# Low parts of experts 5 to 7 moved behind the attention loop, its tail reordered, and one-pass count products

## The chip, the core and the metric

The kernel runs on one core of a Trainium2 chip. Its engines work side by side, each through its own list of instructions in order, and wait for one another by semaphores: TensorE (PE, with its weight loads as PEld), VectorE (DVE), ScalarE (ACT), GpSimd (POOL) and SyncE (SP), which issues transfers. The metric is the time of one execution on the device, in microseconds, as the median of several runs.

## What is computed

The input is 16 images of 16 x 16 positions with 192 channels, 4096 tokens. Three blocks follow one another, each added to its input:

```python
xs = gelu(x @ W1.T + b1)                # 192 -> 48
xs = abs(ifft2(fft2(xs) * low_mask))    # low pass over the 16 x 16 positions
x = x + xs @ W2.T + b2
t = x.reshape(16, 256, 192)
n = layernorm(t)
q, k, v = n @ Wq + bq, n @ Wk + bk, n @ Wv + bv     # 12 heads of 16; one k, one v head
t = t + softmax(rope(q) . rope(k) * scale) @ v      # over the heads of one token
n = layernorm(t)
p = softmax(n @ gate_w.T)               # 8 experts
p1, p2, e1, e2 = top2(p)                # gates p1 / (p1 + p2), p2 / (p1 + p2)
t = t + sum over the two: gate * ((silu(n @ G[e]) * (n @ U[e])) @ D[e])    # 192 -> 384 -> 192
```

As there is one key and one value head and the sum runs over the key heads of the same token, attention is a product of each token with itself. Results are float32; many products are made from a high part in fp32r and a low part (the rest), so that several one-pass products stand for one float32 product.

## The kernel before

The kernel is a hand-written program: each engine's list is written out, with its waits. The tokens lie in 32 tiles of 128, four tiles to a quad, eight quads (`QUADS`, numbered 0 to 7; `last` is 7). There are three phases, each a block that all engines leave together before the next begins.

**The front phase** (`front_phase`) makes the low pass block and then attention. Its attention loop runs over the quads, n = 0 to 7, on every engine. PE projects quad n + 1 (`project`), transposes quad n + 2 (`turn`), makes the gate logits of quad n - 4 (`logits`) and transposes the normalised rows of quad n - 3 (`turn_route`). DVE makes the scores of quad n (`scores`), adds attention to the rows of quad n - 1 and takes their statistics (`residual`), and makes the weights of quad n from ACT's exponentials (`weights`: L756, L758, L761). POOL rotates the key of quad n + 1 (`rotate_key`), weighs the value of quad n (`weigh_value`, L640) and makes the deviation and shift of quad n - 1 (`deviation`, L650 to L659). ACT copies out of PSUM, exponentiates (`exponential`), normalises rows for the gate (`norm_route`, L513, four instructions a quad) and copies logits into `lg` (`copy_logits`, L495). SP stores the normalised rows and the base of the output.

Into this loop the preparation of the experts' weights is woven. For each of the 8 experts ACT makes high parts: `wa_hi` and `wb_hi` (gate and up weights, 128 x 768 each; ACT's `split`) and the first half of `wd` (down weights, 128 x 576; ACT's `split_down`). The low parts are subtractions: `wa` by POOL's `split` (L613), `wb` by DVE's `split` (L729), and the down weights by POOL's `split_down` (L619) for experts 0 to 4 and by DVE's `split_down` (L734) for 5 to 7. POOL makes the `wa` of experts 0 to 3 ahead of the loop and 4 to 7 in its steps 0 to 3, then the down parts of 0 to 3 in steps 4 to 7 and of 4 at the end. DVE makes the `wb` of expert 0 ahead of the loop and of n + 1 in step n, and the down parts at the end of step 7 and behind the last residual.

**The tail of the front phase** finishes the gate logits of quads 4 to 7. When those of quads 0 to 5 are in `lg` (`EARLY`, 24 tiles) DVE makes the early choice (`choose_experts` on these tiles): its maximum and first subtraction (L843) let ACT exponentiate (L563); probabilities, the two best experts, `both` (which of the 8 experts are chosen, 0 or 1) and the gates follow, some twenty small instructions in a chain. ACT's list orders its end of the work: normalise quad 6, copy the logits of 4, copy quad 5's transposes out of PSUM, copy the logits of 5, exponentiate for the early choice, normalise 7, and then 6 and 7 in turn.

**The routing phase** (`routing_phase`) makes the choice for the last 8 tiles, then counts with two products over `both` (L960 with a triangle of ones for the places, L961 with a square of ones for the totals), and from these the order of the tokens by expert (`idx_map`). **The experts' phase** gathers 71 tiles of 128 rows, runs them through their experts and adds the results to the output.

Of the kernel before, what the change touches and what calls it, by code (L numbers as in the profile page):

```python
# [54 lines left out]
EPS = 1e-5  # L55
WARM = 4
ROUTE_APART = (5, 7)
SCALE = HD ** -0.5
# [29 lines left out]
def program(nc, x, xT, w1, w2, lowpass, wqkv, cos, sin, gate, wgu, down, tri, ident, iotas, ytab, out):  # L88
# [4 lines left out]
    with ExitStack() as whole:  # L93
# [41 lines left out]
        with ExitStack() as middle:  # L135
            choice = [middle.enter_context(nc.sbuf_tensor(n, [P, TILES, EXPERTS], F32)) for n in ("pr", "m1", "m2", "both", "gates", "desc")]
            front_phase(nc, early, xs, shift, rstd, eye, wa_hi, wb_hi, w_lo, wd, wqa, wqb, cos_t, sin_t, gate_w, lg, choice, rows, row_tiles,
                        x, xT, w1, w2, lowpass, wgu, down, ytab, ident, wqkv, gate, rope, iotas[1], out)
            routing_phase(nc, lg, choice, tri, iotas, row_tiles, idx_map, tile_exp, switch, out, scattered)
# [19 lines left out]
def front_phase(nc, early, xs, shift, rstd, eye, wa_hi, wb_hi, w_lo, wd, wqa, wqb, cos_t, sin_t, gate_w, lg, choice, rows, row_tiles,  # L159
# [6 lines left out]
    with ExitStack() as stack:  # L166
# [62 lines left out]
        with nc.Block() as block:  # L229
# [65 lines left out]
            def _(pe):  # L295
# [123 lines left out]
                for n in range(QUADS):  # L419
# [6 lines left out]
                    if n >= LAG:  # L426
                        turn_route(n - LAG)
                for q in range(QUADS - LAG, QUADS):
                    turn_route(q)
                    logits(q - 1)  # L430
                logits(last)

            @block.scalar
            def _(act):
# [58 lines left out]
                def copy_logits(q):  # L493
                    act.wait_ge(lg_mm_done, made(q))
                    nc.scalar.activation(lg[:, bass.ts(q, QT), :],  # L495
                                         route_banks(q)[1][:, bass.ds(2 * P, QT * EXPERTS)].rearrange("p (t e) -> p t e", t=QT),
                                         ACT.Copy).then_inc(lg_done, 1)
# [42 lines left out]
                for n in range(QUADS):  # L540
# [15 lines left out]
                    for e in DOWN_AT.get(n, ()):  # L556
                        split_down(e)
                norm_route(last - 1)
                copy_logits(last - 3)
                route_out_of_psum(last - 2)  # L560
                copy_logits(last - 2)
                act.wait_ge(early_less, 1)
                nc.scalar.activation(pr[:, 0:EARLY], lg[:, 0:EARLY], ACT.Exp).then_inc(early_ex, 1)  # L563
                norm_route(last)
                route_out_of_psum(last - 1)
                copy_logits(last - 1)
                route_out_of_psum(last)
                copy_logits(last)

            @block.gpsimd  # L570
            def _(pool):
# [89 lines left out]
                for q in range(QUADS - 1):  # L661
                    in_deviation(q)
                    if 1 < q < QUADS - 2:
                        split(q - 2)
                rotate_key(0)
                in_deviation(last)
                for n in range(QUADS):
                    if n + 1 < QUADS:
                        rotate_key(n + 1)
                    if n < EXPERTS - 4:  # L670
                        split(4 + n)
                    weigh_value(n)
                    if n:
                        deviation(n - 1)
                    if n > 3:
                        split_down(n - 4)
                deviation(last)
                split_down(4)

            @block.vector  # L680
            def _(dve):
# [45 lines left out]
                def split(e):  # L727
                    dve.wait_ge(hi_done, e + 1)
                    nc.vector.tensor_tensor(wb_lo[:, e, :], wb_lo[:, e, :].bitcast(F32), wb_hi[:, e, :].bitcast(F32), ALU.subtract)  # L729

                def split_down(e):
                    dve.wait_ge(down_hi_done, e + 1)
                    low = wd[:, e, 1, :]
                    nc.vector.tensor_tensor(low, low.bitcast(F32), wd[:, e, 0, :].bitcast(F32), ALU.subtract)  # L734

# [60 lines left out]
                finish(last)  # L796
                split(0)
                for n in range(QUADS):
                    scores(n)
                    if n:  # L800
                        residual(n - 1)
                    weights(n)
                    if n + 1 < EXPERTS:
                        split(n + 1)
                    if n + 1 == QUADS:
                        split_down(5)
                residual(last)
                split_down(6)
                split_down(7)

# [63 lines left out]
def routing_phase(nc, lg, choice, tri, iotas, row_tiles, idx_map, tile_exp, switch, out, scattered):  # L874
# [3 lines left out]
    with ExitStack() as stack:  # L878
        a = Scope(nc, stack, "route")
        trit = a.sb("trit", [P, P])  # L880
        ones, zero = a.sb("ones", [P, P]), a.sb("zero", [P, C])
        io = a.sb("io", [P, P])
        first = a.sb("first", [P, E, T])
# [21 lines left out]
        diff_done, ex_done = a.sem("diff_done"), a.sem("ex_done")  # L905
        chain = a.sem("chain")
        chosen, counted, gates_done = a.sem("chosen"), a.sem("counted"), a.sem("gates_done")
# [3 lines left out]
        with nc.Block() as block:  # L911
# [20 lines left out]
            def _(act):  # L932
                act.wait_ge(diff_done, 1)
                nc.scalar.activation(pr[:, EARLY:T], lg[:, EARLY:T], ACT.Exp).then_inc(ex_done, 1)
                act.wait_ge(consts_in, 16 * len(consts))

                def token_at(i, s):
# [14 lines left out]
            def _(pe):  # L952
                pe.sem_inc(map_done, HR)
                pe.wait_ge(consts_in, 16 * len(consts))


                pe.wait_ge(chosen, 1)
                pe.wait_ge(filled, 1)
                flat = both[:].rearrange("p t e -> p (t e)")
                nc.tensor.matmul(ps_p[:, 0:T * E], trit[:], flat, start=True, stop=True)  # L960
                nc.tensor.matmul(ps_t[:, 0:T * E], ones[:], flat, start=True, stop=True).then_inc(counted, 1)  # L961

# [465 lines left out]
```

## Time and profile before

| what | us |
|---|---|
| median of 3 runs | 410.3 (410.09 to 413.22) |
| the profiled execution | 411.45 |
| its span | 409.4 |
| attention loop, first scores to last residual | 53.73 to 115.52 |
| early choice of experts | 121.87 to 130.83 |
| routing phase | from 133.1 |
| experts' phase | from 166.1 |

The profile is one execution; its times are microseconds from the start of the span. An instruction's row gives its start, its time, engine and line, the operation, what it writes and reads, with sizes (partitions x elements), how many were merged into the row, and in brackets the idle time of its engine just before and what ended it. Where an engine can't start an instruction because a port is taken, that waiting is inside the instruction's own time.

### The profile page before, as it was taken

What the parts mean: (1) busy time and instruction counts of PE and PEld (TensorE: products, weight loads), DVE (VectorE), ACT (ScalarE), POOL (GpSimd) and SP (SyncE); (2) the same over time, 40 slices, a digit from 0 to 9 for tenths busy, and PEclk for the clock granted to TensorE, in tenths of its full rate; (3) what the DMA queues carried; (4) which work ended last, traced back from release to release, by engine and by line L of the source; (5) the groups of instructions that cost most, each with busy time, mean ns of one, the idle gap of its engine ahead of it and who ended that gap; (6) DMA issues with size and microseconds to landing.
All of it is one profiled execution on the core that took longest, in us unless ns stands there. A gap on an engine that the chain in (4) does not pass through costs nothing.

```text
span 409.4 us, 8455 instructions
## 1 busy us (share of the span) xinstructions
PE 348.5 (85%) x2162; PEld 333.8 (82%) x2163; DVE 269.5 (66%) x734; ACT 220.0 (54%) x536; POOL 265.2 (65%) x273
## 2 busy tenths in 40 slices
PE   6988675997656249799999999999999999999990
PEld 5887565887656149789999999999999999999980
DVE  2477988999856799256666656665666566656650
ACT  3485655777523059145555555555555555555540
POOL 3048577868770200347878878788787888888763
PEclk9998999698555555699999999999999999999995
DMA  6999640234442400114544445444444444444432
GB/s 173 291 338 383 221 161 1 91 125 146 138 133 91 84 1 0 53 41 71 73 75 80 71 69 77 71 80 71 69 76 70 82 69 70 76 73 79 71 38 29
DMA packets 39418, 41.07 MB, mean 100 GB/s; under 512 B 13789, under 2 KB 32448, under 8 KB 39392
## 3 DMA queue, kind: packets, MB, share of 16 engines
q0 software_dynamic: 13824, 16.98, 25.5%
q1 hardware_dynamic: 25568, 23.79, 18.6%
q8 instruction: 10, 0.16, 0.2%
q14 instruction: 16, 0.13, 0.1%
HBM read 25.78 MB, written 14.98 MB: 100 GB/s over the span
## 4 chain that ended last, share of the span: by engine, by line
PE 55%; DMA 1%; issue 1%; POOLq 0%; DVE 0%; POOL 0%; ACT 0%; SPq 0%; ACTq 0%; DVEq 0%
PE moe_ps_y L1151 10%; PE moe_ps_h L1137 6%; PE moe_ps_gt L1126 3%; PE moe_ps_gt L1130 3%; PE moe_ps_gt L1127 3%; PE moe_ps_u L1126 3%; PE moe_ps_gt L1129 3%; PE moe_ps_u L1129 3%; PE moe_ps_gt L1128 3%; PE moe_ps_y L1153 3%; PE moe_ps_u L1128 3%; PE moe_ps_u L1127 3%; PE moe_ps_u L1130 3%; PE moe_ps_x L1118 2%; PE moe_ps_x L1117 2%; PE moe_ps_y L1150 2%
## 5 line engine op out<-in xcount | busy, mean ns | idle before, releaser
L1090 POOL DMA_INDIRECT out<-moe_y,idx_map x71 | 113.0, 1592 | 29.3 <-issue 19.5
L1082 POOL DMA_INDIRECT moe_xt<-rows,idx_map x71 | 69.9, 984 | 56.7 <-POOLq L911 30.5
L1234 ACT ACTIVATE moe_yy<-moe_ps_y,moe_xt 128x384 f32<-128x384 f32 x71 | 41.3, 581 | 70.7 <-PE moe_ps_y L1151 70.7
L1151 PE MATMUL moe_ps_y<-wd,moe_h_hi 128*128 x213 | 70.2, 354 | 0.6 <-DVE moe_h_lo L1297 0.6
L1305 DVE TENSOR_TENSOR moe_y<-moe_yy 128x192 f32<-128x192 f32 x71 | 25.5, 360 | 56.1 <-ACT moe_yy L1234 56.1
L1214 ACT ACTIVATE moe_x_hi<-moe_ps_x 128x256 fp32r<-128x256 f32 x71 | 27.3, 385 | 33.9 <-PE moe_ps_x L1118 33.9
L1297 DVE TENSOR_TENSOR moe_h_lo<-moe_ps_h,moe_h_hi 128x384 fp32r<-128x384 f32 x71 | 39.6, 558 | 2.7 <-ACT moe_h_hi L1226 0.5
L1151 PEld LDWEIGHTS moe_ps_y<-wd,moe_h_hi 128*128 128x128 f32 x213 | 40.2, 189 | 1.2 <-issue 1.2
L1281 DVE TENSOR_TENSOR moe_x_lo<-moe_ps_x,moe_x_hi 128x128 fp32r<-128x128 f32 x71 | 20.7, 292 | 30.9 <-ACT moe_x_hi L1214 30.9
L1291 DVE TENSOR_TENSOR moe_hid<-moe_ps_u,moe_sg 128x384 f32<-128x384 f32 x71 | 38.9, 548 | 0.0
L1153 PE MATMUL moe_ps_y<-wd,moe_h_lo 128*128 x142 | 35.5, 250 | 0.0
L1226 ACT ACTIVATE moe_h_hi<-moe_ps_h 128x384 fp32r<-128x384 f32 x71 | 34.9, 492 | 0.5 <-PE moe_ps_h L1137 0.5
L1137 PE MATMUL moe_ps_h<-eye,moe_hid 128*128 128x128 f32 x213 | 34.9, 273 | 0.0
L1220 ACT ACTIVATE moe_sg<-moe_ps_gt 128x384 f32<-128x384 f32 x71 | 34.6, 487 | 0.0
L1126 PE MATMUL moe_ps_u<-wa_hi,moe_x_hi 128*128 x71 | 29.9, 421 | 0.0
L1153 PEld LDWEIGHTS moe_ps_y<-wd,moe_h_lo 128*128 128x128 f32 x142 | 26.9, 189 | 0.0
L356 PE MATMUL front_ps_c<-wqa,front_xa 128*128 128x232 f32 x64 | 19.7, 390 | 8.3 <-ACT front_xb L476 8.3
L1137 PEld LDWEIGHTS moe_ps_h<-eye,moe_hid 128*128 128x128 f32 x213 | 25.4, 141 | 0.2
L1126 PE MATMUL moe_ps_gt<-wa_hi,moe_x_hi 128*128 x71 | 24.2, 341 | 0.7 <-DVE moe_x_hi L1284 0.7
L1130 PE MATMUL moe_ps_gt<-w_lo,moe_x_hi 128*128 x71 | 24.0, 338 | 0.0
L1129 PE MATMUL moe_ps_u<-wb_hi,moe_x_hi 128*128 x71 | 24.0, 338 | 0.0
L1128 PE MATMUL moe_ps_u<-wa_hi,moe_x_lo 128*128 x71 | 24.0, 337 | 0.0
(228 smaller groups left out, 963.1 us busy)
## 6 DMA issues: line engine op xcount, KB each, us to landing
w_lo<-in_wgu SPq DMA_DIRECT2D x8, 768.0 KB, 15.0
xs<-in_x SPq DMA_DIRECT2D x8, 388.0 KB, 8.8
rows<-front_xr SPq DMA_DIRECT2D x8, 384.0 KB, 2.7
out<-xs SPq DMA_DIRECT2D x8, 384.0 KB, 3.5
wd<-in_down SPq DMA_DIRECT2D x8, 288.0 KB, 4.5
xta<-in_xT SPq DMA_DIRECT2D x8, 256.0 KB, 5.1
moe_xt<-rows,idx_map POOLq DMA_INDIRECT x71, 2.8
out<-moe_y,idx_map POOLq DMA_INDIRECT x71, 3.6
```

The lines of the kernel that those rows point to most:

```text
L1082: nc.gpsimd.indirect_dma_start(xt[:, slot, :], None, rows.ap(), bass.IndirectOffsetOnAxis(ap=idx_map[:, j, 0:1], axis=0)).then_inc(gathere ...
L1090: nc.gpsimd.indirect_dma_start(out, bass.IndirectOffsetOnAxis(ap=idx_map[:, j, 1:2], axis=0), y[:, j % YR, :], None, compute_op=ALU.add).t ...
L1126: nc.tensor.matmul(at, x_hi[:, s, 0:P], wa_hi[:, e, w], start=True, stop=False)
L1128: nc.tensor.matmul(at, x_lo[:, s, :], wa_hi[:, e, w], start=False, stop=False)
L1129: nc.tensor.matmul(at, hb, wb_hi[:, e, w], start=False, stop=False)
L1130: nc.tensor.matmul(at, hb, w_lo[:, e, 1, w], start=False, stop=True).then_inc(done, 1)
L1137: ins = nc.tensor.transpose(ps_h[:, bass.ts(k, P)], hid[:, s, bass.ts(k, P)], eye[:])
L1151: ins = nc.tensor.matmul(both, hi, halves, start=(k == 0), stop=(k == 2))
L1153: nc.tensor.matmul(first, lo, high, start=False, stop=False)
L1234: nc.scalar.activation(yy[:, s].rearrange("p h c -> p (h c)"), ps_y[:, s, 0:2 * C], ACT.Copy, scale=xt[:, slot, bass.ds(GC + e, 1)]).then_ ...
L1291: nc.vector.tensor_tensor(hid[:, s, :], ps_u[:, s, 0:HID], sg[:, s, :], ALU.mult).then_inc(hid_done, 1)
L1297: nc.vector.tensor_tensor(h_lo[:, s, :], ps_h[:, 0:HID], h_hi[:, s, :].bitcast(F32), ALU.subtract).then_inc(h_lo_done, 1)
```

## The change

`READY = 5` splits the experts into 0 to 4 and 5 to 7. The `wa` and down low parts of 5 to 7 all become POOL's, in one run after its last deviation; their `wb` low parts become DVE's, in one run after the last residual and ahead of the early choice. POOL's down parts of 0 to 4 come in steps 2 to 6, and DVE's `wb` parts of 0 to 4 in steps 0 to 4. In the tail PE makes the logits of quad 4 ahead of the transposes of 5, and transposes 6 and 7 ahead of the logits of 6 and 7; ACT copies the logits of 4 and 5 ahead of normalising 6, and both transposes ahead of the last two copies of logits. In the routing phase `both` and copies of the two constant matrices are of type fp32r; ACT makes these copies once the constants are in.

```diff
+READY = 5
-            choice = [... [P, TILES, EXPERTS], F32)) for n in ("pr", "m1", "m2", "both", "gates", "desc")]
+            choice = [... [P, TILES, EXPERTS], F32R if n == "both" else F32))
+                      for n in ("pr", "m1", "m2", "both", "gates", "desc")]
...
             # front phase, PE, after the loop
-                for q in range(QUADS - LAG, QUADS):
-                    turn_route(q)
-                    logits(q - 1)
+                logits(last - 3)
+                turn_route(last - 2)
+                logits(last - 2)
+                turn_route(last - 1)
+                turn_route(last)
+                logits(last - 1)
                 logits(last)
...
             # front phase, ACT, after the loop
-                norm_route(last - 1)
                 copy_logits(last - 3)
                 route_out_of_psum(last - 2)
                 copy_logits(last - 2)
+                norm_route(last - 1)
                 act.wait_ge(early_less, 1)
                 nc.scalar.activation(pr[:, 0:EARLY], lg[:, 0:EARLY], ACT.Exp).then_inc(early_ex, 1)
                 norm_route(last)
                 route_out_of_psum(last - 1)
+                route_out_of_psum(last)
                 copy_logits(last - 1)
-                route_out_of_psum(last)
                 copy_logits(last)
...
             # front phase, POOL
-                    if 1 < q < QUADS - 2:
+                    if 1 < q < min(READY + 2, QUADS - 2):
                         split(q - 2)
...
-                    if n < EXPERTS - 4:
+                    if n < READY - 4:
                         split(4 + n)
                     weigh_value(n)
                     if n:
                         deviation(n - 1)
-                    if n > 3:
-                        split_down(n - 4)
+                    if QUADS - 1 - READY <= n < QUADS - 1:
+                        split_down(n - (QUADS - 1 - READY))
                 deviation(last)
-                split_down(4)
+                for e in range(READY, EXPERTS):
+                    split(e)
+                    split_down(e)
...
             # front phase, DVE (its split_down is gone)
-                split(0)
                 for n in range(QUADS):
                     scores(n)
                     if n:
                         residual(n - 1)
                     weights(n)
-                    if n + 1 < EXPERTS:
-                        split(n + 1)
-                    if n + 1 == QUADS:
-                        split_down(5)
+                    if n < READY:
+                        split(n)
                 residual(last)
-                split_down(6)
-                split_down(7)
+                for e in range(READY, EXPERTS):
+                    split(e)
...
             # routing phase, ACT, after the Exp and the wait for the constants
+                act.wait_ge(filled, 1)
+                nc.scalar.activation(oner[:], ones[:], ACT.Copy)
+                nc.scalar.activation(trir[:], trit[:], ACT.Copy).then_inc(exact, 1)
...
             # routing phase, PE
+                pe.wait_ge(exact, 1)
                 pe.wait_ge(chosen, 1)
-                pe.wait_ge(filled, 1)
                 flat = both[:].rearrange("p t e -> p (t e)")
-                nc.tensor.matmul(ps_p[:, 0:T * E], trit[:], flat, start=True, stop=True)
-                nc.tensor.matmul(ps_t[:, 0:T * E], ones[:], flat, start=True, stop=True).then_inc(counted, 1)
+                nc.tensor.matmul(ps_p[:, 0:T * E], trir[:], flat, start=True, stop=True)
+                nc.tensor.matmul(ps_t[:, 0:T * E], oner[:], flat, start=True, stop=True).then_inc(counted, 1)
```

## Rows read from the trace of the kernel before

**Rows 1.** Stages: stretch, length, busy time (instructions) by engine, PE's clock, DMA.
```profile
111.00:133.00 22.00, 13.55 (x64) 13.17 (x62) 13.04 (x37) 6.91 (x19) 9.49 (x12) 0.50 0.42 125
...
166.00:409.00 243.00, 230.64 (x1506) 226.19 (x1506) 140.36 (x357) 128.13 (x286) 182.87 (x142) 0.97 0.43 69
```

**Rows 2.** Timeline of the attention loop, DVE and POOL (columns as told above).
```profile
64.56 1.82 POOL L613 TENSOR_TENSOR w_lo<-w_lo,wa_hi 128x768 fp32r<-128x768 f32 x1
65.27 1.15 DVE L756 TENSOR_SCALAR front_den<-front_ex 128x48 f32<-128x48 f32 x1
...
95.80 0.16 DVE L756 TENSOR_SCALAR front_den<-front_ex 128x48 f32<-128x48 f32 x1
...
96.60 0.95 DVE L729 TENSOR_TENSOR w_lo<-w_lo,wb_hi 128x768 fp32r<-128x768 f32 x1
97.47 1.39 DVE L741 SCALAR_TENSOR_TENSOR front_prod<-front_ps_c,rstd,front_kk 128x192 f32<-128x192 f32 x4
```

**Rows 3.** Timeline, places where DVE and POOL both work on SBUF.
```profile
58.16 1.08 DVE L729 TENSOR_TENSOR w_lo<-w_lo,wb_hi 128x768 fp32r<-128x768 f32 x1
58.39 2.54 POOL L613 TENSOR_TENSOR w_lo<-w_lo,wa_hi 128x768 fp32r<-128x768 f32 x1
...
60.88 1.64 POOL L640 TENSOR_TENSOR front_pv<-front_wt,front_kv 128x384 f32<-128x384 f32 x2
61.56 0.22 DVE L750 TENSOR_TENSOR front_diff<-front_score 128x48 f32<-128x48 f32 x1
...
115.44 2.60 DVE L734 TENSOR_TENSOR wd<-wd 128x576 fp32r<-128x576 f32 x2
115.44 1.98 POOL L619 TENSOR_TENSOR wd<-wd 128x576 fp32r<-128x576 f32 x1
...
119.80 1.41 POOL L619 TENSOR_TENSOR wd<-wd 128x576 fp32r<-128x576 f32 x1
```

**Rows 4.** Timeline of PE, transposes and logits of quad 3.
```profile
100.12 1.51 PE L373 MATMUL front_ps_f<-eye,front_xr 128*128 128x128 f32 x6 [0.78 <-issue]
102.59 2.74 PE L385 MATMUL front_ps_f<-gate_w,front_ra 128*128 128x16 f32 x12 [0.96 <-ACT front_ra L504]
```

**Rows 5.** Timeline from the last residual to the early choice, DVE and ACT.
```profile
112.73 0.96 DVE L767 TENSOR_TENSOR xs<-xs,front_pv 128x768 f32<-128x768 f32 x1 [1.52 <-POOL front_pv L640]
115.61 1.86 ACT L513 ACTIVATE front_xr<-xs,shift,rstd 128x192 f32<-128x192 f32 x4 [5.61 <-POOL shift L659]
121.57 0.20 ACT L495 ACTIVATE lg<-front_ps_w 128x32 f32<-128x32 f32 x1 [3.28 <-PE front_ps_w L385]
121.87 0.35 DVE L835 TENSOR_REDUCE front_prod<-lg 128x24 f32<-128x192 f32 x1 [3.83 <-ACT lg L495]
122.26 0.36 DVE L843 TENSOR_TENSOR lg<-lg,front_prod 128x192 f32<-128x192 f32 x1
122.92 1.84 ACT L513 ACTIVATE front_xr<-xs,shift,rstd 128x192 f32<-128x192 f32 x4
```

**Rows 6.** Timeline of the end of the front phase and the routing phase's first DVE instruction.
```profile
125.73 0.36 DVE L853 TENSOR_TENSOR m<-desc,front_prod 128x192 f32<-128x192 f32 x1
130.47 0.36 DVE L871 TENSOR_TENSOR gates<-front_prod 128x192 f32<-128x192 f32 x1
132.63 0.20 ACT L495 ACTIVATE lg<-front_ps_w 128x32 f32<-128x32 f32 x1 [2.83 <-PE front_ps_w L385]
133.13 0.22 DVE L835 TENSOR_REDUCE route_red<-lg 128x8 f32<-128x64 f32 x1 [2.30 <-PEq L229]
```

**Rows 7.** Timeline of the counts, and one-pass products of the experts' phase.
```profile
137.89 1.22 PE L960 MATMUL route_ps_p<-both,route_trit 128*128 128x256 f32 x2 [5.30 <-DMA route_no_place<-in_iota]
138.96 0.23 DVE L871 TENSOR_TENSOR gates<-route_tmp 128x64 f32<-128x64 f32 x1
140.00 0.42 DVE L994 COPY route_tot<-route_ps_t 128x256 f32<-128x256 f32 x1 [0.81 <-PE route_ps_t L961]
166.86 3.86 PE L1184 MATMUL moe_ps_gt<-wa_hi 128*128 128x384 f32 x11 [2.17 <-PEq L911]
```

More of the change, by code:

```diff
@@ L135, in program @@
         with ExitStack() as middle:
-            choice = [middle.enter_context(nc.sbuf_tensor(n, [P, TILES, EXPERTS], F32)) for n in ("pr", "m1", "m2", "both", "gates", "desc")]
+            choice = [middle.enter_context(nc.sbuf_tensor(n, [P, TILES, EXPERTS], F32R if n == "both" else F32))
+                      for n in ("pr", "m1", "m2", "both", "gates", "desc")]
             front_phase(nc, early, xs, shift, rstd, eye, wa_hi, wb_hi, w_lo, wd, wqa, wqb, cos_t, sin_t, gate_w, lg, choice, rows, row_tiles,
@@ L729, in split @@
                     nc.vector.tensor_tensor(wb_lo[:, e, :], wb_lo[:, e, :].bitcast(F32), wb_hi[:, e, :].bitcast(F32), ALU.subtract)
[L731 to L734, printed above, removed]
                 def scores(q):
@@ L881, in routing_phase @@
         ones, zero = a.sb("ones", [P, P]), a.sb("zero", [P, C])
+        trir, oner = a.sb("trir", [P, P], F32R), a.sb("oner", [P, P], F32R)
         io = a.sb("io", [P, P])
@@ L905, in routing_phase @@
         diff_done, ex_done = a.sem("diff_done"), a.sem("ex_done")
-        chain = a.sem("chain")
+        chain, exact = a.sem("chain"), a.sem("exact")
         chosen, counted, gates_done = a.sem("chosen"), a.sem("counted"), a.sem("gates_done")
```

## The prediction

> **What bounds the kernel now.** I read the stages first [rows 1]. The experts' stage takes 243 us with PE busy for 230.64 of them; no edit touches it, so it moves as a block. The change lies in the three stages before it. In the 22 us between the last attention quad and the choice of experts PE is busy for 13.55, DVE for 13.04, ACT for 6.91 and POOL for 9.49, at a granted clock of 0.50: nothing is saturated, a chain of waits sets that stretch. Then I followed who waits for whom. ACT stands 5.61 us until POOL's shift of quad 6 comes, at 115.61, and only after that normalisation copies the logits of quads 4 and 5; the second copy (121.57) releases DVE, which had stood 3.83 us, for the early choice at 121.87 [rows 5]. Its first two operations let ACT exponentiate and then normalise quad 7 (122.92), and from there transposes, copies and logits run to ACT's last copy at 132.63 + 0.20 = 132.83; DVE's choice had ended at 130.47 + 0.36 = 130.83. The routing stage's first DVE instruction comes 0.30 later, at 133.13 [rows 6].
>
> **The loop.** GpSimd's low parts of experts 5 to 7 leave steps 1 to 3 for the tail. There each holds up a small DVE instruction: L756 takes 1.15 us at 65.27, until the 1.82 us L613 of 64.56 is over, where it takes 0.16 at 95.80 [rows 2]. There are three such, so 3 x about 0.96 = 2.9 us. GpSimd's down halves now come two steps earlier, at the same place in the step as that of the 95.80 pattern, which cost nothing. DVE's own low parts move by one index (split(0) from before the loop to step 0), so steps 0 to 4 keep one each; steps 5 and 6 lose theirs, worth 97.47 - 96.60 = 0.87 each [rows 2]. DVE is busy nearly all of the step, so this counts, but POOL then binds almost as much, and I take 0.75 each: 1.5 us. DVE's down half after the last weights, a subtraction of 0.7 us, no longer holds POOL's product L640 ahead of the last residual (1.64 for its two instructions unhindered [rows 3]): I take 0.3. Sum 4.7 (bounds: 1.0 if only the first stall counts, 5.0). The last residual, 112.73 in [rows 5], would start near 108.0 and end, with its statistics, near 110.8.
>
> **Logits of quad 5.** PE and ACT run a ring of their own beside this loop (transposes of quad 3 at 100.12, logits at 102.59) [rows 4]. Only the first stall surely moves it; so I start those transposes at 98.9, 1.2 earlier. From there, by those rows: 1.51 for transposes, 0.96 until logits start, 2.74 for logits, three times over, 15.6 us; with a copy and a turn-round of 0.3 each, quad 5's logits are in SBUF near 115.3, against 121.77. The new order (copies of 4 and 5 ahead of the normalisation of 6, logits of 4 ahead of the transposes of 5) takes POOL's shift off this chain. If the ring follows the whole loop's gain, it is up to 2 us earlier; then DVE's three moved low parts are last, 110.8 + 3 x 0.95 and a little for POOL between them = 113.9. Those three would lie in idle time in either case. POOL's two normalising sequences run meanwhile, hindered by them, until 114.4 to 115.2 (middle 114.8).
>
> **The tail.** Here is what the change pays. POOL's six instructions, 3 x 1.82 (L613) + 3 x 1.41 (L619) = 9.7 us [rows 2, 3], now run beside the early choice, made mostly of DVE instructions with two SBUF inputs. Such pairs exclude each other: POOL's L613 of 58.39 took 2.54 instead of 1.82, as it first stood behind DVE's L729 of 58.16; and of two DVE subtractions at 115.44, which by size (576 elements, at 0.95 us for the 768 of L729) are worth 0.7 each, the pair took 2.60: POOL's L619, asking from the same moment, waited for the first (1.98 instead of 1.41) and then held up the second [rows 2, 3]. So they alternate, and each POOL instruction lets one DVE instruction pass. One row speaks against it: L750, two inputs from SBUF, took its plain 0.22 in the midst of POOL's L640 [rows 3]. The port is free some 0.12 us before an instruction's recorded end ([rows 2]: 65.27 + 1.15 - 0.16 = 66.26 against L613's end at 66.38).
>
> The walk: POOL's first low part has the port from 114.8 to 116.5; the choice's maximum runs beside it and L843 passes at 116.5; ACT, free of quad 6's normalisation at 117.0, exponentiates until 117.35. Then, one DVE instruction after each: POOL to 118.0 (before DVE's next), 119.8 (L847), 121.3 (L850), 123.3 (L851), 124.8 (L853). What follows L853 is unhindered and takes what it takes now, 130.83 - 126.09 = 4.74 [rows 6]. DVE's early choice ends near 125.14 + 4.74 = 129.9. Bounds: 129.0 with the early logits, 131.4 with POOL from 115.2 and the port held to each recorded end. ACT normalises quad 7 from 117.4 to 119.3; with both evictions before the copies, transposes 1.6, two logits of 2.7 and a copy end near 126.5, 7.2 after it where it is now 8.07 (132.83 less the 124.76 at which L513 of [rows 5] ends). So DVE's choice is last, POOL's work ends near 124.9, and the routing stage starts at 130.2 instead of 133.13: 2.9 us.
>
> The Trainium skill, SBUF — State Buffer, section Who interferes with whom, has a rule that speaks against the change: a DVE instruction with two SBUF inputs contends with a GpSimd instruction that reads SBUF, the one that issues first having the shared port for its whole length. By it the end is the one just worked out; by L750 alone it would be 126.5, rival B. The page doesn't say who is next when both wait.
>
> **One-pass counts.** Now PE starts the two count products at 137.89, released by the last constant, and DVE reads them at 140.00, 0.81 after its gates are done at 139.19 [rows 7]. New on the path are two ACT copies of 128x128 behind the constants: bounds 0.20 (128x32) [rows 6] and 0.46 each (a quarter of the 1.86 us L513) [rows 5]; 0.5 for both. The products drop from 2.1 us to one-pass forms: 384 such columns took 3.86 / 11 = 0.35 [rows 7], so 2 x 0.25 and some 0.2 of latency for 256. 137.89 + 0.5 + 0.7 = 139.1, so DVE's gates at 139.2 become last: 0.75 (0.4 to 0.8). `both` in another type and the semaphores cost nothing I can see: the writes are of the same size. The tables that they need lie ahead in the same queue, so no DMA is added.
>
> **Sum.** 2.9 + 0.75 = 3.7 us off the profiled execution, 411.45 (a span of 409.4 and 2.05 around it), thus 407.75; the median of the runs is 1.15 below that execution: 410.3 - 3.7 = **406.6**.
>
> **Rivals.**
> A, the forecast, the two engines alternate at the port: bounds 129.0 to 131.4 give 405.7 to 408.1.
> B, the small DVE instructions are not held (L750): then ACT's last copy at 126.5 ends the stage, 6.3 + 0.75 = 7.1 less, 403.2. Against it: the three stalls of L756, also a short instruction.
> C, POOL, with its queue full, keeps the port from one instruction to the next, and L843 waits for all six: 114.8 + 9.7 = 124.5. Exponential, normalisation and 7.2 us follow: 134.3, 1.5 later than now, less 0.75 for the counts: 411.0, slower. It decides as soon as L843 comes after 123.9 (its present 122.26 and the 0.87 and 0.75 that the tail order and the counts save). Against it: L613 of 58.39, ready in POOL's queue, stood behind the L729 that had asked 0.23 before it [rows 3].
> D, the loop's gain stays small because exponentials wait in ACT behind copies of logits: they would be ready only 0.1 to 0.7 us ahead of DVE's need in steps 5 to 7 by my walk. With 1.0 instead of 4.7 us the whole tail comes 3.5 later, DVE ends at 133.4, and the counts' 0.75 barely cancels it: 410.1, no change.
>
> **How the numbers follow.** A 0.62, B 0.13, C 0.07, D 0.18. About 1% (4.1 us) is what a measurement of this kernel can tell from no change; that bound, 406.2, lies inside A. Its early half (DVE's end before 129.5) is 0.28 of the 0.62, which with B gives 0.41 for faster by over 1%; C would have to grow by a further 3.4 us to be slower by over 1%, 0.04; the rest, 0.55, is within it. The range takes A whole, B, and about half of D: 403.0 to 409.2, leaving out C and the rest of D. A's own range is 405.7 to 408.1.
>
> **What would show it.** L756 at 0.16 in all steps and the last residual near 108: the loop. Logits of quad 5 copied near 113 to 115.5, ahead of quad 6's normalisation: the new order. DVE instructions of the early choice at 1.3 to 2 us instead of 0.36, one to each POOL subtraction: A; all at 0.36: B; L843 alone at several us: C. The last to end before the routing stage is DVE in A, ACT in B and C. The first count product 0.5 later after the stage's start, and DVE's read of it 0.75 earlier: the counts. The forecast is wrong if POOL's low parts start much before 114 (then more of them lie in idle time and the gain grows), or if ACT's and PE's ring, not DVE, sets the loop.

## The result, and the profile after

| what | before | after |
|---|---|---|
| median, us (19 runs each) | 410.30 | 406.87 |
| ratio, with its 95% interval | 1 | 0.9886 (0.9859 to 0.9914) |
| the profiled execution, its span | 411.45, 409.4 | 404.54, 402.6 |

The ratio, taken without the few executions that ran in a slower state (three of after), is a gain of 4.7 us (3.5 to 5.8), where the medians of all 19 differ by 3.4. That is faster by about 1%; the interval, 0.86% to 1.41%, doesn't say whether by more or less than that. The forecast was 406.6 us.

The two profiled executions differ by 6.8 us of span, and not all of that is the change. Up to the second scores the execution of after was the quicker one: they begin at 56.54 us, against 59.16 before. The one edit there is that DVE's first low part (`split(0)`) is gone from before the loop. It stood in front of a wait of DVE (0.69 us for POOL's key at 53.73), though POOL's product beside it took 1.09 instead of 0.32; in the kernel with the order alone, which still has it, 1.45 us of waiting follow it. What it cost can't be told apart here, since from run to run of the kernels below the start of the second scores lies anywhere from 56.5 to 60.8, with or without it. So I measure from the second scores to the experts' first product: 107.70 us before and 103.45 after, a gain of 4.25. From that product to the end it is 242.54 (409.4 less the 166.86 of [rows 7]) and 242.61. The second scores of before, and later steps' scores, from DVE's timeline:

```profile
59.16 1.38 DVE L741 SCALAR_TENSOR_TENSOR front_prod<-front_ps_c,rstd,front_kk 128x192 f32<-128x192 f32 x4
...
90.56 1.39 DVE L741 SCALAR_TENSOR_TENSOR front_prod<-front_ps_c,rstd,front_kk 128x192 f32<-128x192 f32 x4
...
104.41 1.39 DVE L741 SCALAR_TENSOR_TENSOR front_prod<-front_ps_c,rstd,front_kk 128x192 f32<-128x192 f32 x4
```

The two stages that [rows 1] showed, now from views of stages of the kernel after (columns as there):

```profile
104.50:126.50 22.00, 11.55 (x52) 10.59 (x51) 18.98 (x37) 7.06 (x18) 17.07 (x16) 0.50 0.40 120
159.99:402.60 242.61, 231.10 (x1506) 226.45 (x1506) 140.10 (x357) 127.50 (x286) 182.62 (x142) 0.97 0.42 69
```

DVE's 13.04 us in the 22 us of the tail have become 18.98, though only about 1 us of work was added for it; the rest is waiting, since what an engine waits at the port stands inside its instructions' own times (the tail below shows it). POOL's 9.49 have become 17.07, most of it its four further subtractions. The loop after, from the timeline of DVE (start, time, line, operation, what it writes and reads):

```profile
56.54 1.38 DVE L743 SCALAR_TENSOR_TENSOR front_prod<-front_ps_c,rstd,front_kk 128x192 f32<-128x192 f32 x4
...
62.64 0.15 DVE L758 TENSOR_SCALAR front_den<-front_ex 128x48 f32<-128x48 f32 x1
...
84.17 0.95 DVE L736 TENSOR_TENSOR w_lo<-w_lo,wb_hi 128x768 fp32r<-128x768 f32 x1
85.04 1.39 DVE L743 SCALAR_TENSOR_TENSOR front_prod<-front_ps_c,rstd,front_kk 128x192 f32<-128x192 f32 x4
...
91.12 1.39 DVE L743 SCALAR_TENSOR_TENSOR front_prod<-front_ps_c,rstd,front_kk 128x192 f32<-128x192 f32 x4
...
97.53 1.39 DVE L743 SCALAR_TENSOR_TENSOR front_prod<-front_ps_c,rstd,front_kk 128x192 f32<-128x192 f32 x4 [0.28 <-POOL front_kk L635]
...
105.82 0.96 DVE L769 TENSOR_TENSOR xs<-xs,front_pv 128x768 f32<-128x768 f32 x1 [2.16 <-POOL front_pv L645]
```

The stall of [rows 2] at 65.27 (1.15) is gone, here and in the other steps. Steps 5 and 6, without a low part, last 6.08 (91.12 - 85.04) and 6.41, against 6.91 (97.47 - 90.56) and 6.94 before; in the second one the engine already waits 0.28 for POOL's keys. The last residual stands 49.28 behind the second scores, against 53.57 [rows 5].

The tail, from the timelines of ACT, POOL and DVE:

```profile
109.08 0.20 ACT L500 ACTIVATE lg<-front_ps_w 128x32 f32<-128x32 f32 x1 [2.83 <-PE front_ps_w L387]
109.18 1.86 ACT L518 ACTIVATE front_xr<-xs,shift,rstd 128x192 f32<-128x192 f32 x4
...
112.45 1.80 POOL L618 TENSOR_TENSOR w_lo<-w_lo,wa_hi 128x768 fp32r<-128x768 f32 x1
113.01 1.46 DVE L846 TENSOR_TENSOR pr<-pr,front_prod 128x192 f32<-128x192 f32 x1
114.22 1.52 POOL L624 TENSOR_TENSOR wd<-wd 128x576 fp32r<-128x576 f32 x1
114.50 0.35 DVE L834 TENSOR_REDUCE front_prod<-pr 128x24 f32<-128x192 f32 x1
114.89 1.06 DVE L849 TENSOR_TENSOR front_prod<-pr,front_prod 128x192 f32<-128x192 f32 x1
115.69 1.93 POOL L618 TENSOR_TENSOR w_lo<-w_lo,wa_hi 128x768 fp32r<-128x768 f32 x1
115.98 1.85 DVE L850 TENSOR_TENSOR front_prod<-front_prod,desc 128x192 f32<-128x192 f32 x1
...
121.11 0.20 ACT L500 ACTIVATE lg<-front_ps_w 128x32 f32<-128x32 f32 x1 [2.36 <-PE front_ps_w L387]
121.62 1.05 DVE L857 TENSOR_TENSOR front_prod<-front_prod 128x192 f32<-128x192 f32 x1
125.88 0.36 DVE L870 TENSOR_TENSOR gates<-front_prod 128x192 f32<-128x192 f32 x1
126.56 0.22 DVE L834 TENSOR_REDUCE route_red<-lg 128x8 f32<-128x64 f32 x1 [0.32 <-PEq L231]
```

The logits of quad 5 are copied ahead of quad 6's normalisation, no longer 6 us behind POOL's shift as in [rows 5] (121.57, where the shift released the normalisation at 115.61). Then the two engines take turns: six subtractions of POOL, and for each one instruction of DVE that lasts 1.05 to 1.85 us where it takes 0.36 alone. Together the six are 6.2 us longer than alone (1.10 + 0.70 + 1.49 + 0.70 + 1.48 + 0.69). The reduces between them, with one input, keep their 0.35, and so does the reciprocal at 112.67 its 0.30. (One input is no rule, though: L756, held for 1 us in [rows 2], has one by its row.) ACT's last copy is over at 121.31, DVE's choice at 126.24: the choice ends the phase, the other way round than in [rows 6].

### The profile page after: what moved, and what is told of

It reads as the page before. It is cut to its first block, busy times and chain, and to the rows that moved or that the text cites. A ratio compares the mean times of both kernels' runs of the same rounds, so it can differ in the third digit from the quotient of the medians.

```text
span 402.6 us, 8457 instructions
## 1 busy us (share of the span) xinstructions
PE 343.7 (85%) x2160; PEld 329.2 (82%) x2161; DVE 268.0 (67%) x731; ACT 220.3 (55%) x538; POOL 268.0 (67%) x276
## 4 chain that ended last, share of the span: by engine, by line
PE 57%; DMA 1%; issue 0%; POOLq 0%; POOL 0%; ACT 0%; DVE 0%; SPq 0%; ACTq 0%; DVEq 0%
PE moe_ps_y L1154 10%; PE moe_ps_h L1140 6%; PE moe_ps_gt L1129 3%; PE moe_ps_gt L1133 3%; PE moe_ps_gt L1130 3%; PE moe_ps_u L1129 3%; PE moe_ps_gt L1131 3%; PE moe_ps_u L1132 3%; PE moe_ps_gt L1132 3%; PE moe_ps_y L1156 3%; PE moe_ps_u L1131 3%; PE moe_ps_u L1130 3%; PE moe_ps_u L1133 3%; PE moe_ps_x L1120 2%; PE moe_ps_x L1121 2%; PE moe_ps_y L1153 2%
```

## The experiments

Each kernel is read by the same stretches, in us; all places are counted from its own second scores. "Choice" is the early choice on DVE.

| kernel | last residual | choice starts | its length | choice ends | last copy ends | routing starts | experts' first product |
|---|---|---|---|---|---|---|---|
| before | 53.57 | 62.71 | 8.96 | 71.67 | 73.67 | 73.97 | 107.70 |
| after | 49.28 | 54.58 | 15.12 | 69.70 | 64.77 | 70.02 | 103.45 |
| order alone | 53.54 | 58.77 | 9.64 | 68.41 | 69.61 | 69.91 | 103.83 |
| low parts alone | 49.45 | 58.59 | 12.33 | 70.92 | 69.66 | 71.25 | 105.08 |
| after, without the six | 49.27 | 54.56 | 8.96 | 63.52 | 64.75 | 65.05 | 98.35 |
| after, fills for the six | 49.26 | 54.56 | 9.60 | 64.16 | 64.93 | 65.90 | 99.21 |
| after, own semaphore | 49.28 | 54.58 | 15.13 | 69.71 | 64.76 | 70.03 | 102.90 |
| earlier splits | 55.81 | 59.84 | 9.84 | 69.68 | 70.22 | 70.81 | 104.12 |
| placed otherwise | 51.07 | 56.44 | 10.01 | 66.45 | 67.21 | 67.89 | 100.74 |
| six among the experts | 49.43 | 54.73 | 9.30 | 64.03 | 64.91 | 65.76 | 98.88 |

**Order alone.** The kernel before, with the new order of PE and ACT only:

```diff
-                for q in range(QUADS - LAG, QUADS):
-                    turn_route(q)
-                    logits(q - 1)
+                logits(last - 3)
+                turn_route(last - 2)
+                logits(last - 2)
+                turn_route(last - 1)
+                turn_route(last)
+                logits(last - 1)
...
-                norm_route(last - 1)
                 copy_logits(last - 3)
                 route_out_of_psum(last - 2)
                 copy_logits(last - 2)
+                norm_route(last - 1)
...
```

> Only the new order of PE's and ACT's lists behind the attention loop, in the kernel before; low parts and counts as before. I read the stretch S from DVE's second group of scores to the experts' first product: 107.7 us in the kernel before, 103.45 in the changed one. Theory T (order and moved low parts each gain, but not together, as the moved ones hold up the early choice at the SBUF port): quad 5's logits are copied near 116.3 instead of 121.6, DVE's down halves end at 118.0, the choice starts there, quad 7 is normalised from 119.9 (POOL's shift) and ACT's last copy ends near 129: 3.8 less, S = 103.9. Rival G (the gain of the change is the loop's 4.3, the order alone saves what it saves behind the last normalisation, 0.9): S = 106.8.

Measured: 0.9885 (0.9840 to 0.9931) to the kernel before, 103.83, as theory T had it. The order alone gives nearly as much as the whole change: 3.87 of the 4.25 us of the stretch, and a ratio that can't be told from it.

**Low parts alone.** The kernel before with the moved low parts, old order, old counts:

```diff
             # POOL, behind its last deviation; the rest as in the change
-                split_down(4)
+                for e in range(READY, EXPERTS):
+                    split(e)
+                    split_down(e)
...
```

> Only the moved low parts (READY = 5 on POOL and DVE), with the old order behind the loop and the old counts. Theory T: the loop is 4.3 shorter as in the changed kernel, quad 5's logits are copied 6 us after POOL's shift of quad 6 as before, five of POOL's six subtractions each hold one DVE instruction of the early choice, which ends last: 2.4 less than before, S = 105.3. Rival G (the loop's gain arrives whole): S = 103.4. If S is near 107.7, the moved low parts give back all that they gain.

Measured: 0.9946 (0.9914 to 0.9978), 105.08, theory T again. So the parts don't add: 3.87 for the order and 2.62 for the low parts, but 4.25 for both with the counts. DVE's and POOL's timelines of this kernel say why:

```profile
114.81 1.81 POOL L615 TENSOR_TENSOR w_lo<-w_lo,wa_hi 128x768 fp32r<-128x768 f32 x1
116.57 1.40 POOL L621 TENSOR_TENSOR wd<-wd 128x576 fp32r<-128x576 f32 x1
...
117.71 0.47 DVE L839 TENSOR_TENSOR lg<-lg,front_prod 128x192 f32<-128x192 f32 x1
...
119.33 0.73 DVE L843 TENSOR_TENSOR pr<-pr,front_prod 128x192 f32<-128x192 f32 x1
```

With the old order DVE waits for logits until 117.32, and POOL's first two subtractions lie in that time, holding DVE up by 0.11; the whole choice is held 3.4 us (12.33 - 8.96). The new order brings the choice forward into all six, and it is held 6.2.

**After without POOL's six subtractions** (the low parts of experts 5 to 7 that POOL makes are left out, so the output is off):

```diff
                 deviation(last)
-                for e in range(READY, EXPERTS):
-                    split(e)
-                    split_down(e)
```

> The changed kernel without POOL's six subtractions in the tail: the low parts of wa and of the down weights of experts 5 to 7 are left as they were loaded, so their part of the output is off. Theory T (these six hold up the early choice): its instructions take 0.36 again, DVE ends 7.8 us after the exponential, ACT's last copy of logits ends the phase, 4.9 us earlier than in the changed kernel: S = 98.5. Rival (the long instructions of the choice have another cause, or another wait is right behind): S = 102.5 to 103.5.

Measured: 0.9789 (0.9756 to 0.9823), 98.35, theory T; the choice takes 8.96, as in the kernel before. The six cost 5.1 us where the change puts them. Without them ACT's last copy ends the phase, so of the 6.2 us that DVE is held 1.2 only take up what it would have waited for ACT.

**Earlier splits.** The kernel before with order and counts of after; POOL's low parts of experts 5 to 7 stay in the loop, ahead of the keys instead of behind them, and one down part moves:

```diff
+                    if 0 < n < EXPERTS - 4:
+                        split(4 + n)
                     if n + 1 < QUADS:
                         rotate_key(n + 1)
-                    if n < EXPERTS - 4:
-                        split(4 + n)
+                    if n == 0:
+                        split(4)
+                    if n == last:
+                        split_down(3)
                     weigh_value(n)
...
```

> The kernel before with the new order, one-pass counts and its own distribution of low parts, but in steps 1 to 3 POOL subtracts wa ahead of rotating the next key instead of behind it, so that its 1.8 us fall between DVE's residual and DVE's L756; POOL's down part of expert 3 ahead of the last value product, that of 4 behind the last deviation. Theory T (what costs in the loop is only where POOL's long instruction meets a DVE one): L756 takes 0.2 to 0.3 instead of 1.1, the loop is 2.6 shorter, one POOL subtraction meets the early choice, the phase ends near 124.9 on the clock of the kernel before, 7.9 earlier; with the counts' 0.3 S = 99.5, time 402. Rival (POOL is full in steps 1 to 3 and its later keys and shifts cost what the port gives back): S = 102.

Measured: 0.9861 (0.9822 to 0.9901), 104.12: neither theory. The timelines:

```profile
61.25 1.80 POOL L616 TENSOR_TENSOR w_lo<-w_lo,wa_hi 128x768 fp32r<-128x768 f32 x1
61.31 2.55 DVE L774 TENSOR_TENSOR xs<-xs,front_pv 128x768 f32<-128x768 f32 x1 [0.76 <-POOL front_pv L643]
...
79.56 0.17 DVE L763 TENSOR_SCALAR front_den<-front_ex 128x48 f32<-128x48 f32 x1
...
94.71 0.19 DVE L763 TENSOR_SCALAR front_den<-front_ex 128x48 f32<-128x48 f32 x1 [1.10 <-ACT front_ex L494]
...
109.43 1.39 DVE L763 TENSOR_SCALAR front_den<-front_ex 128x48 f32<-128x48 f32 x1
```

Two of the stalls are gone as meant (0.17 at 79.56), but in step 1 POOL asked 0.06 us ahead of the residual and held it for 1.6 us, and the down part put ahead of the last value product cost 1.2 at 109.43, the first instruction of the last weights. In steps 5 and 6 DVE waited 1.10 and 0.74 for exponentials that stood in ACT behind a copy of logits; PE's granted clock in this execution was 0.59, 0.72 and 0.66 in the three stretches of 5 us from 85 on (a mix of its levels of 1.2 and 2.4 GHz), behind one at 1.00 in which PE was busy for 4.67 of 5 us; in the execution of after the same three stretches have 1.00, 1.00 and 0.77. That is rival D's mechanism, seen in one execution; where the clock falls inside the loop differs from one execution to the next, and I didn't try to force it.

**Placed otherwise.** Order and counts of after, POOL's low parts in steps 0, 2 and 3, exponentials ahead of copies of logits, two of DVE's low parts ahead of the first weights, and two down parts of each engine behind its last residual or deviation. Though the text below doesn't name it, the edit also gives the triangle constant its own semaphore, as in the experiment of that name further down:

```diff
+                    if n == 0:
+                        split(4)
+                    if n in (2, 3):
+                        split(4 + n)
                     if n + 1 < QUADS:
                         rotate_key(n + 1)
...
                     weigh_value(n)
+                    if n == 0:
+                        split(5)
...
```

> The kernel before with the new order of TensorE and ScalarE, the one-pass counts, the exponentials ahead of the copies of logits on ScalarE, and the same low parts on the same engines as before, placed otherwise: GpSimd makes those of experts 4 and 5 in step 0, of 6 and 7 ahead of the keys of steps 2 and 3, and the last two down parts behind the last deviation; VectorE makes its first two ahead of the loop and of the first weights, its last two down parts behind the last residual. Theory (what an engine makes in a step costs nothing where the step's stall hides it, and the tail is then free of all but two of GpSimd's subtractions): the three stalls at the weights fall from 0.96 to 0.15 and no other one grows, from the second scores to the experts' first product about 99 us, against 103.45 in the changed kernel, a ratio near 0.980. Rival (the loop has no room left for them, so each subtraction that comes in shows up in a stall at the port or at the weights, as in the run with the earlier splits): 103 to 104 us, a ratio near 0.988.

Measured: 0.9841 (0.9784 to 0.9898), 100.74, between the theory and the rival. Some 0.6 of what it gains on after comes from the semaphore (32.85 from the start of routing to the experts' first product, against 33.43). No stall at the weights is left, as the theory said, but one came elsewhere, and a low part of 0.87 stays in steps 5 and 6.

```profile
60.73 1.80 POOL L616 TENSOR_TENSOR w_lo<-w_lo,wa_hi 128x768 fp32r<-128x768 f32 x1 [0.20 <-ACT wb_hi L468]
61.39 1.21 DVE L758 TENSOR_TENSOR front_diff<-front_score 128x48 f32<-128x48 f32 x1
```

This L758 is the L750 of [rows 3], which took 0.22 amid another POOL instruction; behind a subtraction of POOL it is held 1.0. So it isn't exempt. Why it passed there is not shown; it came, at 61.56, as the first of two merged L640 instructions was ending (60.88 and half of 1.64), which would fit.

**Fills in place of the six.** POOL's six subtractions become fills of the same tiles (the low parts are left out here too):

```diff
-                    split(e)
-                    split_down(e)
+                    pool.wait_ge(hi_done, e + 1)
+                    pool.sem_inc(pool_turn, 1)
+                    nc.gpsimd.memset(wa_lo[:, e, :].bitcast(F32), 0.0)
...
+                    nc.gpsimd.memset(wd[:, e, 1, :].bitcast(F32), 0.0)
```

> The changed kernel, but GpSimd's six subtractions are fills of the same six tiles at the same places, which read nothing from SBUF; the low parts of experts 5 to 7 are thus left out of the result. Theory (VectorE's instructions with two inputs in SBUF are held by a GpSimd instruction that reads SBUF, not by one that only writes it): the choice's instructions of two inputs last 0.36 us each as in the run without the six, and from the second scores to the experts' first product it takes 98.4 us. Rival (any GpSimd instruction at work in SBUF holds them): one instruction of the choice is drawn out by each fill, as far as the fill lasts, and the stretch takes 101 us or more.

Measured in one profiled execution: 99.21, and in the timelines

```profile
116.69 0.58 POOL L689 MEMSET wd<- 128x576 f32 x1
116.83 0.36 DVE L853 TENSOR_TENSOR front_prod<-pr,front_prod 128x192 f32<-128x192 f32 x1
117.22 0.74 POOL L686 MEMSET w_lo<- 128x768 f32 x1
117.23 0.36 DVE L854 TENSOR_TENSOR front_prod<-front_prod,desc 128x192 f32<-128x192 f32 x1
```

Not one instruction of the choice is held, though the fills last only 0.58 and 0.74 us and four of its two-input instructions lie wholly inside one. (The choice is 0.64 longer than without the six, but that is a wait: 1.08 instead of 0.43 for ACT's exponential.) POOL being busy in SBUF is not the cause; it is that its subtractions read there. The Trainium skill, SBUF — State Buffer, section Who interferes with whom, says so: a DVE instruction with two SBUF inputs contends with a GpSimd instruction that reads SBUF and not with one that only writes. Here the trace agrees on both halves, 1.05 to 1.85 us and 0.36.

**A semaphore of its own for the triangle constant.** After, with one edit in the counts:

```diff
-                    sp.dma_start(dst[:], src).then_inc(consts_in, 16)
+                    sp.dma_start(dst[:], src).then_inc(trit_in if dst is trit else consts_in, 16)
...
-                act.wait_ge(consts_in, 16 * len(consts))
+                act.wait_ge(trit_in, 16)
...
```

> The changed kernel, with a semaphore of its own for the triangle constant, so that ScalarE's two copies do not wait for the routing's last constant. Theory (the one-pass counts gained 0.34 us and not 0.75 because the copies start only when all six constants are in): the copies are done before VectorE's gates, and the copy of the totals starts about 6.1 us after the routing stage's first instruction on VectorE (6.53 in the changed kernel, 6.87 before). Rival (the products themselves set it): 6.5 again, with the products late although the copies are early.

Measured in one profiled execution: DVE's copy of the totals comes 5.98 us after the routing stage's first DVE instruction, against 6.53 in after and 6.87 before. In the timelines ACT's copies now come early, and the totals wait for the gates alone:

```profile
130.40 0.31 ACT L937 ACTIVATE route_oner<-route_ones 128x128 fp32r<-128x128 f32 x1 [1.04 <-DMA route_trit<-in_tri]
...
133.34 0.55 PE L961 MATMUL route_ps_p<-both,route_trir 128*128 128x256 f32 x1 [10.26 <-DVE both L861]
...
134.43 0.23 DVE L870 TENSOR_TENSOR gates<-route_tmp 128x64 f32<-128x64 f32 x1
134.57 0.42 DVE L995 COPY route_tot<-route_ps_t 128x256 f32<-128x256 f32 x1
```

**The six among the experts.** After, but VectorE makes the six at the start of the experts' phase, ahead of the first products that could want them whatever the choice of experts:

```diff
             # POOL, behind its last deviation
-                for e in range(READY, EXPERTS):
-                    split(e)
-                    split_down(e)
...
             # DVE, at the start of the experts' phase
+                low = lambda at, hi: nc.vector.tensor_tensor(at, at.bitcast(F32), hi.bitcast(F32), ALU.subtract)
+                for e in range(READY, EXPERTS):
+                    low(w_lo[:, e, 0, :], wa_hi[:, e, :])
                 x_low(0, 0)
+                low(wd[:, READY, 1, :], wd[:, READY, 0, :])
+                low(wd[:, READY + 1, 1, :], wd[:, READY + 1, 0, :])
                 x_low(0, 1)
                 hidden(0, 0)
+                low(wd[:, READY + 2, 1, :], wd[:, READY + 2, 0, :])
```

> The changed kernel, but GpSimd's six subtractions are not made beside the early choice: VectorE makes them at the start of the experts, three ahead of the first low part of x (where it sat idle 3.35 us in the changed kernel), three in the two gaps behind it (2.20 and 1.42 us). The whole computation is there. Theory (the six cost the tail what they hold at the port, and nothing else): from the second scores to the experts' first product 98.4 us, as in the run without the six (98.35; 103.45 with them), and from that product to the end 242.6 us as before, so 5 us less than the changed kernel: a ratio of 0.979 to the kernel before. Rival (the six cost about the same wherever they stand): the tail gains the 5 us, but the stretch from the experts' first product to the end grows by about 6 x 0.8 = 4.8 us to 247, a ratio near 0.988.

Measured: 0.9765 (0.9724 to 0.9807), median 401.12 against 410.96 of the kernel before beside it: quicker than both kernels, its interval below that of after. 98.88 to the experts' first product and 242.94 from it to the end (242.61 in after). DVE's timeline there:

```profile
160.38 2.67 DVE L1307 TENSOR_TENSOR w_lo<-w_lo,wa_hi 128x768 fp32r<-128x768 f32 x3
163.80 0.29 DVE L1281 TENSOR_TENSOR moe_x_lo<-moe_ps_x,moe_x_hi 128x128 fp32r<-128x128 f32 x1 [0.74 <-ACT moe_x_hi L1214]
...
164.45 1.43 DVE L1307 TENSOR_TENSOR wd<-wd 128x576 fp32r<-128x576 f32 x2
```

They lie in idle time: behind the first three DVE still waits 0.74 for ACT, and behind the others 0.82 and 0.74. What ends the front phase here is neither DVE (64.03) nor ACT (64.91): routing starts at 65.76, and the DMA that stores the last of xs, issued at 119.74, takes 5.7 us to land by the view of DMA issues, at 125.4, just ahead of routing's first instruction at 125.94; waiting for it is the last thing in SyncE's list for this phase (0.9 us). That store is the likely next bound; no run moves it.

## Why the forecast came out right

- **Loop**: right in kind, a little small. 4.29 us (53.57 - 49.28) instead of 4.7. The three stalls went entirely (2.9). The steps without a low part gave 0.83 and 0.53 where I had 0.75 each: in the second one POOL's keys bind, as feared. The 0.3 at the last value product did not come: step 7 lasts 8.29 from its scores to the last residual, against 8.32. POOL's two products are shorter there (1.63 instead of 1.96) but begin 0.71 behind the start of the weights' last instruction instead of 0.41; why is not shown.
- **Logits of quad 5**: earlier than either case I gave, without effect. They are in SBUF at 111.9 on the time axis of before (52.74 behind the second scores), where I had 115.3, or up to 2 us less. PE's and ACT's ring did follow the whole loop's gain: quad 3's transposes start at 94.14, which is 96.8 on that axis, not 98.9. And these transposes and logits lasted 0.84 and 1.51 instead of the 1.51 and 2.74 of [rows 4], at a granted clock of 1.00 (94 to 97.5 us) against 0.50 (100 to 105.5 before). So DVE's three moved low parts were last, as in my second case, and the choice began 8.1 us earlier, at 113.7 on the axis of before; I had 113.9.
- **Tail**: A, alternation at the port. By the walk the choice would end at 129.9, at the early bound 129.0; measured 69.70 behind the second scores, 128.9 on the axis of before. POOL started while DVE was between L842 and L846, so the first DVE instruction held was L846 and not the L842 that the walk had named by its number of before, L843; the pattern behind it, one to each subtraction, was that of the walk, with six instructions held where the walk had five. Routing starts 3.95 us earlier, not 2.9; 0.9 of the 1.05 more is what the walk gave to earlier logits (129.0 instead of 129.9).
- **Counts**: the term that was mis-sized, 0.34 instead of 0.75 in the two profiled executions. By my sum DVE's read comes 5.97 behind the stage's first DVE instruction (139.1 - 133.13), just ahead of the end of the gates at 6.05; it came at 6.53. The last constant released the copies at 5.12, where it had released the products at 4.76 before: 0.36. The copies took the 0.5 that I had given them. From their end to the read it was 0.90 instead of 0.7, of which 0.2 (latency) stood on no row:

```profile
131.68 0.31 ACT L937 ACTIVATE route_oner<-route_ones 128x128 fp32r<-128x128 f32 x1 [4.35 <-DMA route_no_place<-in_iota]
131.90 0.29 ACT L938 ACTIVATE route_trir<-route_trit 128x128 fp32r<-128x128 f32 x1
132.29 0.55 PE L963 MATMUL route_ps_p<-both,route_trir 128*128 128x256 f32 x1 [11.21 <-ACT route_trir L938]
132.64 0.41 PE L964 MATMUL route_ps_t<-both,route_oner 128*128 128x256 f32 x1
...
133.09 0.42 DVE L997 COPY route_tot<-route_ps_t 128x256 f32<-128x256 f32 x1 [0.48 <-PE route_ps_t L964]
```

  The gates are done at 132.61, so 0.48 was lost to the products; with the constant's own semaphore that is won back. The time of the constants differs from execution to execution, and this pair shows the least gain: the read comes at 6.23 to 6.53 in the five kernels with these counts and at 6.87 to 7.05 in the three with the old ones, 0.55 apart in the mean. That is still less than 0.75.
- **Sum**: 3.95 + 0.30 (what is left of the counts at the experts' first product) = 4.25, against 3.7 forecast and 4.7 (3.5 to 5.8) timed. That the median, 406.87, lies only 0.27 from the forecast is in part luck: the tail gave 1.05 more and the counts 0.45 less than forecast, and the difference of the medians is itself below the gain of the stretch. DVE's choice ended in A's early half, by which the forecast had a gain of over 1%; whether it was over 1% the timing leaves open.
- **Rivals**: B is out (an instruction of 0.36 is held, six times). C is out: POOL never kept the port for two subtractions while DVE asked. D did not come true; its waits showed only in another kernel's execution.
- What I did not see beforehand is where the gain came from. The forecast is a sum of a loop that gives and a port that takes. But the order alone, which I counted as a means to bring the logits forward, is worth 3.87 of the 4.25. On top of it the low parts and the counts together brought 0.38 (103.83 to 103.45), and none of that is the low parts': routing starts at 70.02 with them and at 69.91 with the order alone, and the 0.49 behind that start (33.92 to 33.43) is the counts'. With the low parts moved the choice begins 4.19 earlier (54.58 for 58.77) and, held at the port, takes 5.48 longer (15.12 for 9.64). Only the runs with one part alone could tell.

## What to carry to other kernels

Work that is moved off a full loop onto another engine is not free where that engine shares a read port with the one that sets the end: count for each moved instruction one held instruction of the other. Look for a stretch where the *other* engine stands idle, however far away, before looking for one where the moving engine does: here six subtractions that cost 5.1 us beside the choice cost at most 1 us in waits of VectorE some 45 us later (98.88 and 242.94 against 98.35 and 242.49 without them). And when a change has two parts that meet in one place, time each alone, since their gains need not add.

## What the runs showed of the hardware that I had not expected

- Turns at the port are strict in the choice of after: six subtractions, and behind each one instruction of DVE that had waited. The waiter starts a little before the other's recorded end: L846, 0.36 long by itself, ended at 114.47, so it began near 114.11, while POOL's subtraction is recorded until 114.25.
- A fill by POOL of the same tile is 0.74 us where the subtraction is 1.80, and it neither holds DVE up nor is held.
- The same code after the second scores repeats closely from execution to execution (last residual 49.26 to 49.43 behind them in after and the four kernels made from it), while the second scores themselves start anywhere from 56.5 to 60.2 in these five. Within one program such a stretch tells apart what the total time can't.
